# Moving DVE, POOL, ScalarE and DMA steps to other slots in a two-layer attention and expert kernel

## The reference, cut to what matters

```python
kv_in = concatenate([layernorm(x[b]), ctx[b]])          # 256 + 1601 = 1857 rows
q = rope(rms_norm(xn @ Wq.T)); k = rope(rms_norm(kv_in @ Wk.T)); v = kv_in @ Wv.T
attn = softmax(q @ k.T) @ v                             # per head, 256 x 1857
x = x + attn @ Wo.T
# for the second layer, which attends to 9 near context rows per token and to their mean:
table[b] = ctx[b] @ [W_kvc | W_kvc @ W_kr], its last 64 columns rotated by position
mean[b]  = mean over the context of ctx[b] @ W_kvc
near     = table[b][first_row[token] : first_row[token] + 9]
```

## Time and profile before

| what | value |
|---|---|
| median of the runs | 1949.68 us |
| profiled execution, its own time | 1947.32 us |
| span of its instructions | 1945.4 us |
| mean granted TensorE clock | 0.943 |
| busy PE, DVE, ACT, POOL | 1723.2, 1457.1, 1087.0, 1122.0 us |

### The profile page before, as it was taken

The page is one execution under the profiler, slowest core; times in us unless marked ns, Lnnn a source line. Parts: engine busy times, 40 slices in busy tenths (PEclk is TensorE's granted clock), DMA queues, the critical chain, the costliest instruction groups (busy, mean ns, idle before and its releaser), DMA issues. The chain is left out here.

```text
span 1945.4 us, 41606 instructions
## 1 busy us (share of the span) xinstructions
PE 1723.2 (89%) x14578; PEld 1314.0 (68%) x14727; DVE 1457.1 (75%) x3802; ACT 1087.0 (56%) x2676; POOL 1122.0 (58%) x1727
## 2 busy tenths in 40 slices
PE   4789898998998999999999899996999999089997
PEld 2578777787777777777778777775555555038974
DVE  7887896877978778788687787865757765675746
ACT  3567667676667666666766666663133333073543
POOL 5686686775857769568576685600256664072210
PEclk7899999999999999999999999996999999586998
DMA  4121110111110102101011100014368896510100
GB/s 137 46 75 40 34 33 12 40 64 37 50 35 9 34 8 95 43 12 44 1 38 49 54 22 12 8 51 185 117 209 269 270 268 191 161 31 16 45 11 26
DMA packets 74777, 140.25 MB, mean 72 GB/s; under 512 B 11177, under 2 KB 45970, under 8 KB 74322
## 3 DMA queue, kind: packets, MB, share of 16 engines
q1 hardware_dynamic: 64594, 107.21, 17.9%
q0 software_dynamic: 9984, 30.42, 4.4%
HBM read 111.73 MB, written 25.86 MB: 71 GB/s over the span
## 5 line engine op out<-in xcount | busy, mean ns | idle before, releaser
L897 DVE TENSOR_TENSOR att_pT<-att_pT 128x512 bf16<-128x512 f32 (+1 forms) x512 | 319.3, 649 | 156.8 <-ACT att_pT L764 153.6
L552 PE MATMUL att_out<-att_V,att_pT 128*128 128x128 bf16 x5760 | 390.8, 220 | 31.9 <-DVE att_pT L897 24.1
L552 PEld LDWEIGHTS att_out<-att_V,att_pT 128*128 128x128 bf16 x5760 | 351.1, 98 | 63.3 <-DVE att_pT L897 23.3
L764 ACT ACTIVATE att_pT<-att_pT 128x512 bf16<-128x512 f32 (+1 forms) x512 | 277.4, 569 | 172.4 <-PE att_pT L540 171.5
L770 ACT ACTIVATE att_prob<-att_scores,att_negmax 128x512 f32<-128x512 f32 (+1 forms) x512 | 330.1, 654 | 36.4 <-DVE att_negmax L886 34.8
L531 PE MATMUL att_scores<-att_K,att_Q 128*128 128x512 bf16 (+1 forms) x1408 | 299.1, 359 | 8.2 <-DVE att_K L859 1.4
L884 DVE TENSOR_REDUCE att_mx<-att_scores 128x1 f32<-128x512 f32 (+1 forms) x512 | 291.1, 628 | 0.6 <-PE att_scores L531 0.6
L540 PE MATMUL att_pT<-att_ident,att_prob 128*128 128x128 f32 x1920 | 276.5, 275 | 0.0
L531 PEld LDWEIGHTS att_scores<-att_K,att_Q 128*128 128x128 bf16 x1536 | 150.7, 98 | 145.3 <-issue 2.6
L453 PE MATMUL att_aux<-att_wkv,att_kvT 128*128 128x256 bf16 x1440 | 185.7, 280 | 36.9 <-DVE att_aT L859 16.3
L540 PEld LDWEIGHTS att_pT<-att_ident,att_prob 128*128 128x128 f32 x1920 | 210.6, 142 | 1.3
(11 more groups left out here) (329 smaller groups left out, 3176.6 us busy)
## 6 DMA issues: line engine op xcount, KB each, us to landing
moe_wa<-in_wa_l SPq DMA_DIRECT2D x80, 480.0 KB
att_wq<-wq_s SPq DMA_DIRECT2D x12, 512.0 KB, 5.3
att_wo<-wo_s SPq DMA_DIRECT2D x12, 512.0 KB, 6.3
moe_y<-y_s SPq DMA_DIRECT2D x8, 768.0 KB, 4.6
near_s<-att_stage POOLq DMA_DIRECT2D x8, 576.0 KB, 3.2
win_near<-near_s SPq DMA_DIRECT2D x32, 144.0 KB
moe_wb<-in_wb_l SPq DMA_DIRECT2D x80, 48.0 KB
att_cst<-in_ctx_l SPq DMA_DIRECT2D x6, 512.0 KB, 4.4
```

The costliest lines, as they stand in the source:

```text
L552: last = nc.tensor.matmul(out_ps[:, i % 2, :], pT[:, i % 2, a, k, :], V[:, par, k, w, :], start=(k, a, w) == (0, 0, 0), stop=(k, a) == (KT ...
L764: nc.scalar.activation(pT[:, i % 2, 0, 4 * j:4 * j + m, :], pT_ps[j % 2][:, 0:m, :], ACT.Copy).then_inc(s["pt_hi"], 1)
L897: nc.vector.tensor_tensor(pT[:, i % 2, 1, 4 * j:4 * j + m, :], pT_ps[j % 2][:, 0:m, :], pT[:, i % 2, 0, 4 * j:4 * j + m, :], ALU.subtract) ...
```

## The change

- DVE's low half of a slot's "ahead" task stands before the third row maximum (in slot 5 before the second), not after the negated maximum.
- MN goes from the end of slot 7 of groups 0, 3, 7, 11 to the head of slot 0 of groups 1, 4, 8, 12.
- The context's split goes from slot 2 to slot 0, but for group 0 and the last group of each batch, where it stays. On ScalarE in slot 0 it stands ahead of high half 2. The column sum comes two slots after the split's low half: slot 2, or slot 4.
- The angle steps go from slots 3 to 7 and 1 to 4 of two groups to slots 0, 3, 7; 3, 7; 0, 3, 6, 7 of three. `normal_rows` goes from slot 0 to slot 1. The sines go from slot 6 of the third group of a batch to slot 0 of the fourth, ahead of high half 2.
- Weight pieces: head 3's K and Q in slot 4 of group 1 (was 1), head 2's O in slot 1 of group 2 (was slot 4 of group 1). POOL makes the low halves of those of slot 4, and turns the table rows, after the last block's rope.
- The gathers come at the end of POOL's work in groups 4, 5, 8, 9, 12, 13, and SP does the stores, each at the head of the next group's list.

```diff
 SLOTS = [
-    ([], [("KV", 0)], [("KV", 1)]),
+    ([("MN", 0)], [("KV", 0)], [("KV", 1)]),
...
-    ([("KT", 2)], [("KT", 3)], [("MN", 0)]),
+    ([("KT", 2)], [("KT", 3)], []),
...
-PIECES_AT = {(0, 1): [(1, "O")], (0, 4): [(2, "K"), (2, "Q")], (1, 1): [(3, "K"), (3, "Q")], (1, 4): [(2, "O")], (2, 4): [(3, "O")]}
+PIECES_AT = {(0, 1): [(1, "O")], (0, 4): [(2, "K"), (2, "Q")], (1, 4): [(3, "K"), (3, "Q")], (2, 1): [(2, "O")], (2, 4): [(3, "O")]}
+NEAR_IN = [KVH * b + m for b in range(1, B) for m in range(2)]
+MEANS_IN = [1] + [KVH * b for b in range(1, B)]
+ANGLES_AT = {(0, 0): 0, (0, 3): 1, (0, 7): 2, (1, 3): 3, (1, 7): 4, (2, 0): 5, (2, 3): 6, (2, 6): 7, (2, 7): 8}
+def keys_slot(g):
+    return 2 if g == 0 or g % KVH == KVH - 1 else 0
... SP's list of a group
+                    if g - 1 in NEAR_IN:
+                        near_out(NEAR_IN.index(g - 1))
                     if g < SPLITS:
                         sp.wait_ge(s["c_sum"], g + 1)
                         next_keys(g + 1)
...
                     if g == 0:
+                        sp.wait_ge(s["w_lo"], 3)
+                        weight_in(2, "K")
+                        weight_in(2, "Q")
                         weight_kept(1, "O")
... ScalarE's slot, between the ahead tasks and high half 2
+                    if i == 0 and not last and g < SPLITS and keys_slot(g) == 0:
+                        keys_high(g)
+                    if i == 0 and not last and g % KVH == KVH - 1 and g < (B - 1) * KVH:
+                        turn_table(g // KVH + 1)
... DVE's row maxima
-                def row_max(tile, i):
+                def row_max(tile, i, ahead, g, u):
                     for k, (lo, n) in enumerate(BANKS):
+                        if k == (1 if i == 5 else 2):
+                            for x_ in ahead:
+                                task(*x_, g, u)
                         dve.wait_ge(s["qk_done"], NB * tile + k + 1)
...
-                        if i == 2:
+                        if i == keys_slot(g):
                             keys_low(g)
-                        if g % KVH == 1 and i == 0:
+                        if i == keys_slot(g) + 2:
+                            keys_sum(g)
+                        if g % KVH == 1 and i == 1:
                             normal_rows(b)
... POOL's prep: after the loop over the ropes
+                    for h, k in PIECES_AT.get((now, 4), ()):
+                        weight_low(h, k)
+                    turn_rows(now)
+                    if now in NEAR_IN:
+                        gather(NEAR_IN.index(now))
```

More of the change, by code:

```diff
@@ L147, in tasks_of @@
         elif kind == "MN":
[L148 to L149 removed]
+            if g in MEANS_IN:
+                found.append((kind, MEANS_IN.index(g), 0))
         elif prep:
@@ L372, in _ @@
                         next_keys(g + 1)
-                    for h, kind, after in ((2, "K", 3), (2, "Q", 3)) if g == 0 else ((2, "O", 7),) if g == 1 else ():
-                        sp.wait_ge(s["w_lo"], after)
-                        weight_in(h, kind)
                     if g == 0:
+                        sp.wait_ge(s["w_lo"], 3)
+                        weight_in(2, "K")
+                        weight_in(2, "Q")
                         weight_kept(1, "O")
                     if g == 1:
-                        weight_kept(3, "K")
-                        weight_kept(3, "Q")
+                        sp.wait_ge(s["w_lo"], 5)
+                        weight_in(3, "K")
+                        weight_in(3, "Q")
+                        weight_kept(2, "K")
+                        weight_kept(2, "Q")
+                    if g == 2:
+                        sp.wait_ge(s["w_lo"], 8)
+                        weight_in(3, "O")
+                        weight_kept(2, "O")
                     n = g + 2
@@ L401, in _ @@
                         turns_for(g + 1)
[L402 to L407, removed]
                     if g == 1:
-                        sp.wait_ge(s["w_lo"], 8)
-                        weight_in(3, "O")
-                        weight_kept(2, "O")
+                        sp.wait_ge(s["w_lo"], 7)
+                        weight_in(2, "O")
+                        weight_kept(3, "K")
+                        weight_kept(3, "Q")
                     if g == 2:
+                        sp.wait_ge(s["w_lo"], 9)
                         weight_kept(3, "O")
[L414 to L417, removed]
+                for n in range(len(NEAR_IN), TT):
+                    near_out(n)
                 sp.wait_ge(s["tb_out"], 16 * groups)
@@ L805, in slot @@
                         task(*x_, g, u)
-                    if i == 2 and g < SPLITS:
+                    if i == 2 and not last and g < SPLITS and keys_slot(g) == 2:
                         keys_high(g)
@@ L990, in slot @@
                     if not last:
-                        row_max(tile, i)
-                    for x_ in ahead:
-                        task(*x_, g, u)
+                        row_max(tile, i, ahead, g, u)
+                    else:
+                        for x_ in ahead:
+                            task(*x_, g, u)
                     if old:
@@ L1076, in prep @@
                                 weight_low(h, k)
-                        if order == 5:
-                            turn_rows(now)
-                            if now == 0:
-                                rstd(slice(2, TT), 2)
-                        if order == 7:
-                            for h, k in PIECES_AT.get((now, 4), ()):
-                                weight_low(h, k)
-                        if now >= KVH and now % KVH == 0:
-                            b = now // KVH - 1
-                            if order in (2, 6):
-                                gather(2 * b + order // 6)
-                            if order in (4, 8):
-                                store(2 * b + order // 8)
+                        if order == 5 and now == 0:
+                            rstd(slice(2, TT), 2)
+                    for h, k in PIECES_AT.get((now, 4), ()):
[3 more added lines that the diff above has]
+                        gather(NEAR_IN.index(now))
                 nc.gpsimd.memset(nhalf[:, :], -0.5).then_inc(s["pad"], 1)
@@ L1124, in _ @@
                 turn_rows(groups - 1)
-                for n in (TT - 2, TT - 1):
+                for n in range(len(NEAR_IN), TT):
                     gather(n)
-                    store(n)
-                pool.wait_ge(s["stored"], 16 * TT)
 E_ALL, TOPK, GRP, TOP_GRP = 32, 6, 4, 2
```

23 lines of the change are left out of this document (13 added, 10 removed).

## The result

| | median us (range) | runs | against before, same chip |
|---|---|---|---|
| before | 1949.01 (1946.01 to 1951.16) | 4 | |
| changed | 1961.09 (1960.76 to 1963.14) | 4 | 1.0065 [1.0048, 1.0083] |

The changed kernel is slower by 12.1 us; +12.2 had been forecast. Its profiled execution took 1960.76 us with a span of 1958.9.

The account below looks back on a forecast made before the run. PE's own work was taken as the floor, with other engines' lateness above it. Extra steps and group 0's stall (-20.5) plus the low halves' order (+32.7) gave +12.2 on 1949.7: 1961 us, range 1930 to 1984.

Parts of the forecast that it names:

- extra steps over plain groups: Time of the fifteen groups above plain ones, from splits, angles, sines, gathers; falls from 53.1 to 32.6 us, group 0's stall included.
- plain groups longer: Low halves between maxima lengthen each plain group by 2.2 us: 30.8 for 14 groups, 1.2 for group 0.
- group 15: The last group, also lengthened by the low halves between the maxima: 0.7 us.
- The stall of group 0: Later column sum delays SP's K and Q loads; ScalarE, then PE wait: 10.4 us plus 1.0 for the clock.
- the clock's 1.0 us: Group 0: PE's clock falls to 0.50 after the stall, costing 1.0 us.
- The rival without the stall: Group 0's stall is absent or short: 1950.5 us in all, chance 0.10.
- the sines: Slot 0 of groups 3, 7, 11: table loads and sines delay ScalarE's work, 1.9 us each, 5.7 in all.
- The order of the low halves: Slots 1, 4, 5, 6, 7: low halves between maxima delay exponentials and high half 3; 2.2 us a plain group, +32.7.
- The swallowed delay: DVE's 0.96 us lateness in slot 4 vanishes at the query squares, which end when POOL's instruction ends.
- the rival of 1976: DVE's slot 4 delay passes into slots 5 and 6: 3.2 us a group, +14, chance 0.16.
- the rival in which the order costs nothing: PE's own work covers the later exponentials, so the maxima's order is free: 1929 us, 1945 with half the cost; chance 0.26.
- part 3: Loss from low halves between the maxima in slots 1, 4, 5, 6, 7 of every group: +32.7 us.

Follow-up runs that it names:

- e1: Changed kernel, with SyncE loading head 2's K and Q before it waits for the column sum: 1950.69 us, 1.0015 of the kernel before.
- e2: Changed kernel, with the low half of the ahead task back behind the negated maximum: 1905.12 us, 0.9781 of the kernel before.
- e3: Changed kernel, with K and Q loads before the column-sum wait and the ahead low half back behind the negated maximum: 1897.03 us, 0.9734 of before.
- e4: Kernel before, with the low halves between the row maxima as the only edit: 1977.16 us, 1.0144 of before.
- e12: Kernel before, with POOL's table rotation behind the last rope and the low halves between the maxima: 1971.06 us, 1.0141 of before.
- e9: Kernel before, with POOL's table rotation behind the last rope of the group as the only edit: 1925.76 us, 0.99 of before.
- e5: Changed kernel, with K and Q loads before the column-sum wait and the ahead low half before the fourth maximum in all slots: 1918.29 us, 0.9853 of before.

## Why the prediction was right, and where it was not

The groups' sum makes the comparison. Fifteen groups took 1184.1 us before and 1194.8 after.

| term | forecast | measured | how |
|---|---|---|---|
| extra steps over plain groups | 53.1 to 32.6: -20.5 | 53.1 to 27.8: -25.3 | 1194.8 - 15 x 77.8 |
| plain groups longer | +32.0 | +36.0 | 15 x (77.8 - 75.4) |
| group 15 | +0.7 | +2.4 | 54.5 to 56.9 |
| sum | +12.2 | +13.1 | profiled executions: +13.4 |

The sign and both mechanisms were right. That the total came within 0.1 us is luck: the gain was 4.8 us larger than forecast and the two losses together 5.7 larger, and the misses cancelled.

**The stall of group 0** was right in place, cause and size: 11.4 forecast, 10.4 and 8.1 by e1 and e2 to e3. The trace has every link, 1.1 us late at the DMA issue. The clock's part stands in windows over the stall and behind it. In the stall PE is 2.6 us busy in 13.7, and the granted clock of the stretch is 0.68, between its two levels of 1.2 and 2.4 GHz; it is at the lower level, 0.50, in the stretch in which PE starts again, and back at 1.00 from 134 us on:

```profile
114.20:127.90 13.70, 2.59 (x14) 1.20 (x13) 5.36 (x21) 1.58 (x3) 12.73 (x21) 0.68 0.43 134
127.90:130.00 2.10, 0.57 (x3) 0.60 (x4) 1.43 (x3) 2.00 (x6) 0.00 (x0) 0.50 0.00 0
130.00:134.00 4.00, 4.00 (x38) 3.83 (x37) 3.21 (x9) 1.50 (x3) 0.00 (x0) 0.64 0.01 4
134.00:138.00 4.00, 3.77 (x41) 2.99 (x40) 3.34 (x13) 4.00 (x13) 1.98 (x5) 1.00 0.00 0
```

No run prices the clock's 1.0 us by itself.

The rival without the stall, priced at 1950.5, is e1: 1950.7.

**The extra steps.** In e3, with neither loss in it, the groups sum to 1133.8, which is 22.3 over fifteen of its own plain ones (1111.5). The forecast for that was 18.5 and group 0's remaining 2.7: 21.2. Group 0 itself is 5.9 over plain there, so of the 2.3 us that the prediction let go in it hardly any went (80.4 before, 79.9 in e3), and the other fourteen groups make 16.4 and not 18.5. Single terms, slots between negated maxima: a context sum in slot 4, 0.9 forecast, 0.6 found (slot 4 of group 3 is 11.75 against 11.16 in group 14); the mean's matmuls, 1.05 and 1.1 to 1.2 (group 4 is 75.3 against 74.1 to 74.2); the transposes of the next batch's tokens, XT, 1.0 and 0.3 (groups 5 and 9 are at 74.4), too dear; the sines, 1.9 and 1.95 (slot 0 of group 3 is 10.82, of group 14 8.87). ScalarE in group 3, slot 0 of e3 gives that last one row by row:

```profile
297.96 1.28 ACT L770 ACT_TABLE_LOAD   x1
299.25 1.00 ACT L770 ACTIVATE att_tab<-att_tab 128x960 f32<-128x960 f32 x1
...
301.15 0.58 ACT L784 ACTIVATE att_pT<-att_pT 128x512 bf16<-128x512 f32 x1
301.75 1.28 ACT L790 ACT_TABLE_LOAD   x1
303.04 0.69 ACT L790 ACTIVATE att_prob<-att_scores,att_negmax 128x512 f32<-128x512 f32 x1
```

From the first load to the high half it is 3.2 us, as in the earlier trace rows, and the second load puts the exponential off by 1.3 more. Between the load's end at 299.24 and the sine there is 0.01 us here too. The drain of about 1380 ns that the Trainium skill states for a switch of tables (page "ScalarE: Activation LUTs", section "What ACT_TABLE_LOAD costs") does not appear at this place either. By an estimate from that page's figure, two drains in each of three groups, these groups would have lost 8 us more.

**The order of the low halves.** From one slot's first score matmul (L531, after L551) to the next slot's, group 14; the sum is of all eight slots:

| slot | before | after | e3 | forecast net | after - before |
|---|---|---|---|---|---|
| 1 | 9.57 | 10.10 | 9.57 | 0.65 | 0.53 |
| 4 | 9.79 | 10.32 | 9.79 | 0.6 | 0.53 |
| 5 | 9.71 | 9.77 | 9.70 | 0.05 | 0.06 |
| 6 | 9.28 | 10.37 | 8.76 | 0.5 to 0.7 | 1.09 |
| 7 | 8.58 | 8.73 | 7.79 | 0.1 to 0.4 | 0.15 |
| sum | 75.43 | 77.79 | 74.11 | 2.2 | 2.36 |

The column of the forecast has the steps between the latenesses that the prediction names (0.65, then 1.1 to 1.4, then 1.5 in all). It was within 0.12 us of the measured loss in each slot but slot 6, where the loss was about twice what was allowed. In slots 0, 2 and 3 the three kernels agree to 0.01 us.

Slot 6 parts into two. In e4, which has the order alone, it is 9.97: +0.70, as forecast. The other 0.4 comes with the rotation: e12 has 10.38. With the rotation out of its way POOL does other rope steps beside DVE's squares and value low halves at the end of slot 5, and these take longer. DVE in e4, and then in the changed kernel, from the first square to the query's low half:

```profile
1257.19 0.43 DVE L868 SCALAR_TENSOR_TENSOR att_kjunk<-att_kvraw 128x128 bf16<-128x128 f32 x1
...
1258.61 0.28 DVE L868 SCALAR_TENSOR_TENSOR att_kjunk<-att_kvraw 128x128 bf16<-128x128 f32 x1
...
1259.62 0.68 DVE L859 TENSOR_TENSOR att_Q<-att_aux,att_Q 128x512 bf16<-128x512 f32 x1
```
```profile
1239.35 0.58 DVE L890 SCALAR_TENSOR_TENSOR att_kjunk<-att_kvraw 128x128 bf16<-128x128 f32 x1
...
1240.82 0.81 DVE L890 SCALAR_TENSOR_TENSOR att_kjunk<-att_kvraw 128x128 bf16<-128x128 f32 x1
...
1242.64 0.68 DVE L881 TENSOR_TENSOR att_Q<-att_aux,att_Q 128x512 bf16<-128x512 f32 x1
```

The same six steps take 2.43 us in e4, 3.29 in the changed kernel and 3.30 in e12. DVE enters slot 6 that much later, and PE's last values of that slot, which wait for nothing in e4, wait 0.55 us for low half 3. That POOL's place is the reason is read from these traces; no run moves POOL's steps against DVE's by themselves.

**The swallowed delay**, DVE's lateness in slot 4 that was to vanish at the query squares, was right. In slot 4 low half 3 starts 5.08 us after the first maximum, 0.95 more than before (4.13). The first query square then starts 0.95 late and takes 0.43 us instead of 1.39, because POOL's instruction beside it is nearly over:

```profile
1227.66 1.27 POOL L664 TENSOR_TENSOR att_scaled<-att_qraw,att_qw 128x512 f32<-128x512 f32 x1
```

It ends 5.98 us after the first maximum began, where it had been 5.99, and the last query square ends after 8.22 instead of 8.23. In both kernels the first square ends 0.14 to 0.15 us after POOL's instruction. That fits the exclusive lock of the Trainium skill's page "SBUF — State Buffer", section "Who interferes with whom": a wait that ends with another engine's instruction takes up lateness. So the rival of 1976 falls. The same coupling is not always kind: it is what cost the 0.4 us in slot 6.

**What failed: the price of the rival in which the order costs nothing.** The prediction put it at 1929; the kernel without that cost, group 0's stall still in it, is e2, 1905.1. The step at fault is "the 1.1 us of slot 7 are no longer POOL's. What comes late in their place is DVE's low half 2". Its gain was counted in part 3 alone, set off against the order's cost, so that it was nothing where the order costs nothing. In e2 and e3 the plain group is at 74.1, as in e9: 1.3 us under before, and 15 x 1.3 = 19.5 us if every group is counted as a plain one and its extra steps. That makes 1929 into 1910. Of the rest to 1905.1, 1.7 us are extra steps (e2's groups sum to 1142.4, 30.9 over plain and not 32.6), and 1.5 are the lower median of before in that set of runs. Likewise the order's gross cost is 3.7 us a group in the changed kernel and 2.0 in the kernel before, where POOL's wait hid 1.3 of it (PE waits for POOL no longer in group 14 of e4); the last 0.4 is that of slot 6. e12 settles it: 77.8 with both edits, 74.1 with the rotation alone, 77.4 with the order alone. Two edits that end the same slot go together as the later of two ends, not as a sum, and here the pair was even 0.4 us worse than the later one. The net was right because both stood in one term; a reader who took the terms for independent would have missed the 2.7% that lay in the change.

The chance given to slower, 0.62, rested on terms of +32.7 and -20.5; either alone could have been a third out without turning the sign.

What stays open: how the 1.4 us of the later maximum divide between the exponentials, the KV copy and the addition to x (e5 moves all at once); whether the rotation is still worth anything with the order in, since e4 and e12 ran on different chips and the plain group got longer by it; and why group 0 of e3 is 5.9 us over plain.

## What to carry to other kernels

Before an instruction goes between two waits of an engine, ask what that instruction itself waits for: filling DVE's gap between maxima was free only as long as the filler was ready, and here it made 54 more exponentials wait than before, and PE behind them. When a producer's step moves later, look through every in-order queue that waits for its semaphore, SyncE's list first: independent loads belong in front of such a wait. And when two edits of one change touch the waits at the end of the same slot, price each of them with and without the other, as the later of two ends. Look also at what the moved step leaves behind: the work that follows it on its engine now runs beside other work of its neighbour.

## What the runs showed of the hardware that was not expected

- DVE's squares beside POOL's rope made up 0.95 us of DVE's lateness to within 0.02 us: the first took 0.43 us instead of 1.39, the second 0.28 as before, and the third, beside POOL's next instruction, 1.35 in both kernels. At the end of slot 5 the same kind of overlap made six DVE steps 0.86 us longer (2.43 in e4, 3.29 in the changed kernel).
- POOL work in the middle of a chain of short POOL steps costs PE more than its place suggests: 2.35 us moved behind the last rope, on an engine that is 58% busy, made the kernel 1% faster (e9), and PE's waits for POOL at the key transposes went from 16.7 us to 2.9.
- In ScalarE's rows the table switch for the sine is 1.28 us each way, with 0.01 to 0.02 us from its end to the next activation, whether it stands in slot 7 of the kernel before or in slot 0.
